# A transformer layer on one core: the first keys by halves of tokens, the second term order for their sums, GpSimd's pair output one normalisation later, and a routing step moved at the change of stage

## What is computed

```python
# x: (8, 512, 256); all float32
h = layernorm(x); xn = h / norm(h) * sqrt(256) * (gamma + 1)
q, k, v = split(xn @ w_qkv)                    # 16 heads of 64
attn = softmax((q / 8) @ k.T); x = x + merge(attn @ v) @ w_out
h = layernorm(x)
p = softmax(h @ router_w); top = top_k(p, 2); top = top / sum(top)
x = x + (gelu(h @ w1 + b1) @ w2 + b2) * sum(top)
```

## Time and profile before

| | before |
|---|---|
| median of 3 runs | 1160.66 us (1159.94 to 1162.03) |
| the profiled execution | 1159.99 us |
| its span, first to last instruction | 1158.2 us |
| TensorE busy | 1146.1 us, 99% of the span |
| VectorE / ScalarE / GpSimd busy | 87% / 76% / 58% |
| granted TensorE clock in the records | 1.000 |

### The profile page before, as it was taken

The page is one execution under the profiler, slowest core; times in us unless marked ns, Lnnn a source line. Parts: engine busy times, 40 slices in busy tenths (PEclk is TensorE's granted clock), DMA queues, the critical chain, the costliest instruction groups (busy, mean ns, idle before and its releaser), DMA issues.

```text
span 1158.2 us, 26395 instructions
## 1 busy us (share of the span) xinstructions
PE 1146.1 (99%) x9923; PEld 951.4 (82%) x9923; DVE 1006.8 (87%) x1767; ACT 874.8 (76%) x1896; POOL 666.6 (58%) x827
## 2 busy tenths in 40 slices
PE   9999999999999999999999999999999999999999
PEld 6778888888888888888888888888888877788887
DVE  6889888988888888888888888888988988889985
ACT  6888888888888888888888888888888885334432
POOL 6786566655666565656565656565656585323421
DMA  4224112311231123112221213121312135334321
GB/s 124 75 80 110 34 37 70 90 33 36 74 92 38 38 74 92 38 38 74 70 60 37 74 56 75 37 70 31 92 33 67 43 110 152 129 112 141 116 75 38
DMA packets 58270, 82.92 MB, mean 72 GB/s; under 512 B 12576, under 2 KB 34592, under 8 KB 58144
## 3 DMA queue, kind: packets, MB, share of 16 engines
q1 hardware_dynamic: 58144, 81.24, 25.6%
HBM read 31.14 MB, written 16.25 MB: 41 GB/s over the span
## 4 chain that ended last, share of the span: by engine, by line
PE 91%; DVE 2%; ACT 1%; issue 0%; POOL 0%; DVEq 0%; ACTq 0%; POOLq 0%
PE ps L615 34%; PE ps L696 19%; PE ps L681 12%; PE ps L642 10%; PE ps L648 5%; PE ps L854 4%; PE ps L858 2%; PE ps L767 1%; PE ps L766 1%; PE ps L725 1%; PE ps L824 1%; PE ps L859 1%; DVE pT_lo L1207 0%; DVE f_o L1451 0%; POOL pT_hi L1087 0%
## 5 line engine op out<-in xcount | busy, mean ns | idle before, releaser
L1078 POOL TENSOR_SCALAR prob<-prob,rowinv 128x512 f32<-128x512 f32 x512 | 353.2, 703 | 334.0 <-DVE rowinv L1296 333.9
L1207 DVE TENSOR_TENSOR pT_lo<-ps,pT_hi 128x512 fp32r<-128x512 f32 (+1 forms) x384 | 320.5, 862 | 57.7 <-ACT pT_hi L976 57.1
L983 ACT ACTIVATE prob<-ps,negmax 128x512 f32<-128x512 f32 x512 | 347.3, 688 | 16.3 <-DVE negmax L1291 11.8
L1291 DVE TENSOR_REDUCE negmax<-ps 128x2 f32<-128x1024 f32 x256 | 305.8, 1215 | 1.3 <-PE ps L648 1.2
L973 ACT ACTIVATE pT_hi<-ps 128x1024 fp32r<-128x1024 f32 x128 | 131.3, 1026 | 112.4 <-issue 111.0
L681 PEld LDWEIGHTS ps<-identity,prob 64*128 64x128 f32 x4096 | 157.5, 138 | 67.8 <-issue 44.3
L681 PE MATMUL ps<-identity,prob 64*128 64x64 f32 x4096 | 175.6, 225 | 3.2 <-DVE pT_lo L1207 2.1
L642 PE MATMUL ps<-nat 64*128 64x512 f32 x1024 | 170.9, 411 | 1.4 <-ACT prob L983 1.1
L615 PE MATMUL ps<-xT_hi,wbig 128*128 128x512 f32 x514 | 166.6, 405 | 0.2 <-DVE pT_lo L1207 0.2
L976 ACT ACTIVATE pT_hi<-ps 128x512 fp32r<-128x512 f32 x256 | 139.3, 596 | 8.8 <-PE ps L681 0.6
L696 PE MATMUL ps<-pT_hi,vbuf 128*128 128x512 f32 x512 | 138.4, 392 | 0.9 <-DVE pT_lo L1207 0.9
(11 more groups left out here) (116 smaller groups left out, 1988.9 us busy)
## 6 DMA issues: line engine op xcount, KB each, us to landing
att_hi_v<-halves_out SPq DMA_DIRECT2D x128, 128.0 KB, 2.3
att_lo_v<-halves_out SPq DMA_DIRECT2D x128, 128.0 KB, 2.4
blocks_scratch<-xblocks SPq DMA_DIRECT2D x15, 512.0 KB, 2.8
xn<-blocks_scratch SPq DMA_DIRECT2D x60, 128.0 KB, 2.9
xin<-in_x SPq DMA_DIRECT2D x32, 128.0 KB, 3.0
xres<-in_x SPq DMA_DIRECT2D x8, 512.0 KB, 3.5
x_scratch<-xres SPq DMA_DIRECT2D x8, 512.0 KB, 3.3
xin<-x_scratch SPq DMA_DIRECT2D x32, 128.0 KB, 3.2
```

Of the source, the lines that this page charges most:

```text
L983: act.activation(prob[:, n % NPROB, j * SEQ:(j + 1) * SEQ], ps[:, PS_SCORE[n % 2] + j, :], ACT.Exp, bias=negmax[:, n % 4, j:j + 1], accum_ ...
L1078: return pool.tensor_scalar(dst, src, scalar, 1.0, ALU.mult, ALU.mult)
L1207: return dve.tensor_tensor(dst, full, hi, ALU.subtract)
L1291: dve.tensor_reduce(negmax[:, n % 4, :], ps[:, PS_SCORE[n % 2]:PS_SCORE[n % 2] + 2, :], AX.X, ALU.max, negate=True).then_inc(s_max, 1)
```

## The change

Five edits.

1. The transposes of the first xn go by halves of tokens: ("xt", 0) is tokens 0 to 255 for both channel groups, in banks 0 and 1, ("xt", 1) the rest, in banks 7 and 3. ScalarE's and VectorE's parts of xT come in four pieces of 256 columns each, with semaphores of their own. The first keys are two products of 256 tokens, and each product's terms go hi x hi, then weights-hi x xT_lo, then weights-lo x xT_hi (before: weights-lo second).
2. `gain` (128x2) and the low part of first weights 0 move from VectorE to GpSimd, behind its second `powers`. The single matmul of zeros in step -3 is gone.
3. The high part of the values' first weights (`first_weights(2)`) moves on ScalarE from behind the second piece to between the two pieces of the first queries.
4. GpSimd's `attention_out` of pairs 0 to 61 moves from behind `normalise_prob(4p+8)` to behind `normalise_prob(4p+9)`, the next tile. Pairs 62 and 63 stay.
5. At the change of stage VectorE's `turn_logits(1)` stands ahead of `base(0)`, `routing_shift(1)` ahead of the last two output blocks, `routing_weight(1)` behind `turn_input`, and the two `finish` of chunk 0 behind the hidden blocks f = 1 and f = 4 of chunk 1.

```diff
-WARM = {FIRST_STEP: 12, -3: 1}
+WARM = {FIRST_STEP: 12}
+PS_XT = ((0, 1), (7, 3))
 # TensorE
-                for i, j in ((0, 0), (1, 0), (0, 1)):
+                halves_in = 1 if queries.stop <= SEQ // 2 else 2
+                for i, j in ((0, 0), (0, 1), (1, 0)):
                     if (i, j) == (0, 0):
                         pe.wait_ge(s_first_hi, 1)
                     if i == 1:
-                        pe.wait_ge(s_first_lo, 1)
+                        pe.wait_ge(s_first_lo_pool, 1)
                     for k in range(KT):
-                        if j == 0:
-                            pe.wait_ge(s_auxhi, aux_index[("xt", k)] + 1)
-                        else:
-                            pe.wait_ge(s_aux, done_no("xt", k))
+                        pe.wait_ge(s_xt_lo if j else s_xt_hi, KT * (halves_in - 1) + k + 1)
...
-                    for t in range(TT):
-                        if k == 0:
-                            pe.wait_ge(s_xn_first, t + 1)
-                        ins = pe.transpose(bank[:, t * P:(t + 1) * P], xn[:, t, k * P:(k + 1) * P],
-                                           identity[:, :])
+                    for t in (2 * half, 2 * half + 1):
+                        pe.wait_ge(s_xn_first, t + 1)
+                        for k in range(KT):
+                            ins = pe.transpose(ps[:, PS_XT[half][k], t * P:(t + 1) * P], xn[:, t, k * P:(k + 1) * P],
+                                               identity[:, :])
...
-                        ins = first_product(bank, base, slice(0, SEQ))
+                        for half in range(2):
+                            tokens = slice(half * SEQ // 2, (half + 1) * SEQ // 2)
+                            ins = first_product(bank[:, tokens], base, tokens)
 # ScalarE
+                    for k in range(KT):
+                        act.activation(xT[0][:, k, tokens], ps[:, PS_XT[args[0]][k], tokens], ACT.Copy, scale=gain[:, k:k + 1])\
+                            .then_inc(s_xt_hi, 1)
...
                             .then_inc(s_q_first_hi, 1)
+                        first_weights(2)
                         act.wait_ge(s_auxfull, block_no + 1)
...
-                for g in {FIRST_SLOT + 2: (0,), -7: (1, 2)}.get(slot, ()):
+                for g in {FIRST_SLOT + 2: (0,), -7: (1,)}.get(slot, ()):
 # GpSimd
+                if pair_at(step - 2) is not None and step < STEPS:
+                    attention_out(pair_at(step - 2))
                 task = ln_task(2 * step - 1)
...
                     powers(1, slice(2, TT))
+                    pool.wait_ge(s_const, 16 * N_CONST)
+                    pool.tensor_scalar(gain[:, :], gamma_sb[:, :], 1.0, 1.0, ALU.add, ALU.mult).then_inc(s_gain, 1)
+                    first_lo(0)
...
-                if pair_at(step - 1) is not None:
+                if pair_at(step - 1) is not None and step == STEPS:
                     attention_out(pair_at(step - 1))
 # VectorE
+                    for k in range(KT):
+                        dve.wait_ge(s_xt_hi, KT * args[0] + k + 1)
+                        lo(xT[1][:, k, tokens], ps[:, PS_XT[args[0]][k], tokens], xT[0][:, k, tokens], gain[:, k:k + 1])\
+                            .then_inc(s_xt_lo, 1)
...
-                if slot == -10:
-                    dve.wait_ge(s_first_hi, 1)
-                    lo(first_parts[0][1], first_stage[0], first_parts[0][0]).then_inc(s_first_lo, 1)
...
-                            dve.tensor_scalar(gain[:, :], gamma_sb[:, :], 1.0, None, ALU.add).then_inc(s_gain, 1)
...
+                    if c == 1 and f in (1, TT):
+                        finish(0, f // TT)
                 if c >= 1:
                     base(c)
                 if c == 0:
                     routing_shift(0)
                     routing_weight(0)
+                    turn_logits(1)
                     base(0)
...
-                if c + 1 < B:
+                if 1 <= c < B - 1:
                     turn_logits(c + 1)
                 if c == 0:
+                    routing_shift(1)
                     for block_of_out in last_out:
                         aux_done(*block_of_out)
...
-                if c + 1 < B:
+                if c == 0:
+                    routing_weight(1)
+                elif c + 1 < B:
                     routing_shift(c + 1)
-                finish(c, 0)
+                if c >= 1:
+                    finish(c, 0)
```

More of the change, by code:

```diff
@@ L138, in layer_kernel @@
     out_tasks = [task for task in aux_index if task[0] == "out"]
-    other_tasks = [task for task in aux_index if task[0] != "out"]
+    other_tasks = [task for task in aux_index if task[0] not in ("out", "xt")]
     x_v = x.rearrange("b (p t) d -> b p t d", t=TT)
@@ L731, in aux @@
                 begun = kind == "k" and any(block[2] == "out" for block in aux_of(step)[0])
-                same_bank = [j for j in range(block_no) if aux_bank(j) == aux_bank(block_no)]
+                same_bank = [task for task in other_tasks
+                             if aux_index[task] < block_no and aux_bank(aux_index[task]) == aux_bank(block_no)]
                 if begun:
@@ L936, in aux_hi @@
                 if kind == "xt":
-                    k, = args
+                    tokens = slice(args[0] * SEQ // 2, (args[0] + 1) * SEQ // 2)
                     act.wait_ge(s_gain, 1)
-                    ins = act.activation(xT[0][:, k, :], bank, ACT.Copy, scale=gain[:, k:k + 1])
+                    for k in range(KT):
+                        act.activation(xT[0][:, k, tokens], ps[:, PS_XT[args[0]][k], tokens], ACT.Copy, scale=gain[:, k:k + 1])\
+                            .then_inc(s_xt_hi, 1)
+                    return
                 elif kind == "q":
@@ L1226, in aux_done @@
                     lo(nat[:, 0, QL, 0:P], ps[:, PS_Q_FIRST, 0:P], nat[:, 0, QH, 0:P], SCALE).then_inc(s_q_first, 1)
-                dve.wait_ge(s_auxhi, hi_no)
                 if kind == "xt":
-                    k, = args
-                    ins = lo(xT[1][:, k, :], bank, xT[0][:, k, :], gain[:, k:k + 1])
-                elif kind == "q":
+                    dve.wait_ge(s_gain, 1)
+                    tokens = slice(args[0] * SEQ // 2, (args[0] + 1) * SEQ // 2)
+                    for k in range(KT):
+                        dve.wait_ge(s_xt_hi, KT * args[0] + k + 1)
+                        lo(xT[1][:, k, tokens], ps[:, PS_XT[args[0]][k], tokens], xT[0][:, k, tokens], gain[:, k:k + 1])\
+                            .then_inc(s_xt_lo, 1)
+                    return
+                dve.wait_ge(s_auxhi, done_no(kind, *args))
+                if kind == "q":
                     part = nat[:, args[0] % 2]
@@ L1351, in slot_tasks @@
                             ins.then_inc(s_xn, 1)
-                        if step == 8 and b == 0:
-                            dve.wait_ge(s_const, 16 * N_CONST)
-                            dve.tensor_scalar(gain[:, :], gamma_sb[:, :], 1.0, None, ALU.add).then_inc(s_gain, 1)
             for step in range(FIRST_STEP, LAST_STEP + 2):
@@ L1489, in _ @@
                     turn_input(1)
-                if c + 1 < B:
+                if c == 0:
+                    routing_weight(1)
+                elif c + 1 < B:
                     routing_shift(c + 1)
-                finish(c, 0)
-                if c + 1 < B:
+                if c >= 1:
+                    finish(c, 0)
+                if 1 <= c < B - 1:
                     routing_weight(c + 1)
-                finish(c, 1)
+                if c >= 1:
+                    finish(c, 1)
 def kernel(**inputs):
```

36 lines of the change are left out of this document (20 added, 16 removed).

## The result

| | before | after |
|---|---|---|
| median | 1160.75 us (1159.90 to 1162.03, 22 runs) | 1162.49 us (1161.24 to 1163.57, 22 runs) |
| ratio, 95% interval | | 1.0014 (1.0008 to 1.0020) |
| the profiled execution, its span | 1159.99, 1158.2 us | 1163.23, 1161.3 us |
| mean granted clock of an execution | 1.000 in all | 1.000 in 11, 0.999 in 11 |

The change costs 1.7 us (0.9 to 2.3 by the interval), and the forecast was 0.2 us faster than the median of three.

The account below looks back on a forecast made before the run. TensorE was taken as the bound, busy 1146.1 of 1158.2 us. 1159.99 - 0.4 (head) + 0.2 (stage) + 0 (pair output) = 1159.8 us; the profiled run lies 0.67 below the median, so 1160.5 us, range 1159.4 to 1161.6.

Parts of the forecast that it names:

- the change of stage: Chunk 1: two TensorE waits for gelus (0.68 and 0.43 us) become one of about 2 us; cost 0.2 us.
- Pair output: GpSimd's attention output one normalisation later, 62 pairs: worth 0, cost 0, bound 0.05 us a pair.
- over 1 us to spare: GpSimd's later-input steps: work behind the pair output at most 0.4 us later, the following tile having this margin.
- The rival with this sign: Moved pair output gains after all: 0.05 us on 62 pairs, 3 us, giving 1157.4 us; chance 0.03.
- Head: Start of the kernel: first keys' high part at 10.15 us against 10.53, gain 0.4 us, bounds 0.15 to 0.8.
- the collision: In the head: GpSimd's 1.29 us low part of weights 0 getting in front of VectorE's last xn tile.
- the first rival: In the head, GpSimd precedes VectorE's last xn tile: keys at 11.05, 0.5 us later, total 1161.4 us; chance 0.24.
- The spread's data: Change of stage: SP's spread of xn, starting at 997.4, lands at 1001.4 to 1001.8 us, holding up x2_hi(2).
- The clock: In the head, TensorE's clock falls back to 1.2 GHz: 2.65 us more, total 1163.1 us; chance 0.09.

Follow-up runs that it names:

- E3: Kernel before with only VectorE's new order at the change of stage: 1162.13 us, ratio 1.0010.
- E2: Kernel before with only GpSimd's pair output one normalisation later: 1160.16 us, ratio 0.9994.
- E12: Kernel before with the pair's output later only where GpSimd's high part of the next batch's input follows (seven of 64 pairs): 1160.28 us, ratio 0.9990.
- E1: Kernel before with only the head's edits; pair output and stage change as before: 1161.05 us, ratio 1.0003.
- E7: Changed kernel with x2_hi(2) behind the sixth gelu of chunk 1 and GpSimd's first low weights waiting for all four xn tiles: 1162.16 us, ratio 1.0008.
- E4: Changed kernel with one wait more: GpSimd's low part of the first weights starts only behind the last xn tile: 1161.29 us, ratio 1.0009.
- E9: E4 with VectorE's two sums of the last output blocks moved behind the turned blocks: 1160.47 us, ratio 0.9994.
- E6: Changed kernel with nine extra dummy products on TensorE in its 2.63 us wait before up(1,6): 1161.89 us, ratio 1.0008.
- E11: E4 with the old stage order, except both parts of finish(0) behind low parts f = 1 and f = 4 of chunk 1: 1160.30 us, ratio 0.9993.
- E10: E4 with both parts of finish(0) back in front of chunk 1's low parts, router's logits and shift still early: 1162.11 us, ratio 1.0007.
- E5: Changed kernel with x2_hi(2) and its low part behind the sixth gelu of chunk 1, not the fourth: 1162.58 us, ratio 1.0014.

## Why the prediction was wrong, step by step

Three steps failed, and the largest is the change of stage: priced at +0.2 us, measured at +0.85 us in E3's profile, with about 0.7 us more in the median by the fall of the clock.

**Pair output: 0, measured about -0.6 us (E2, not clear of noise by itself) and -1.0 us (E12, clear of it).** The step "worth 0, since nobody waits for that tile" was read from a pair in the middle and from a view of waits of one execution. For the steps with a later input's high part the prediction had "over 1 us to spare". In the old order the first of them had about 0.1: GpSimd's wait was 0.55 us longer in E3 than in before and 1.21 longer in E1, and the step lost 0.45 and 1.1. In before's execution the halves landed 0.99 us after GpSimd was free; in E1's they landed 2.20 us after it, and the step lost 1.1 us. The move protects that step against a late landing, though not wholly (E7 lost 0.26 us). The prediction had the clue that its profiled execution lay 0.67 us below the median, and treated this as spread without asking what is late in the others. The rival with this sign was bounded by 0.05 us for each of 62 pairs, so the place was wrong and not only the size.

**Head: -0.4, measured +0.6 in the profile.** Without the collision (E4) the keys' high part came at 10.16, forecast 10.15, and with it at 11.19, where the first rival had 11.05, with the long xn row that it named. The first agreement is partly luck: E4's xn began 0.18 us earlier than before's, and the same program gave 10.67 in E9. In the mean of the profiles the head without the collision is worth 0.2 us, half of the forecast. What failed was the choice: a margin of hundredths of a microsecond was given 0.42 against 0.24 in the chances. By the profiles it falls on either side, and alone the head came out at +0.25 us, not separable from nothing.

The Trainium skill (SBUF — State Buffer, section "SBUF: two separate sides") says that VectorE and GpSimd share a port pair, which one of them holds for a whole instruction while the other is blocked. The sizes agree: the tile took 1.45 us, 1.04 more than its 0.41, beside a low part of 1.26. By the page whichever starts first gets the pair. By the recorded starts the tile was first, by 0.04 us, so these don't tell who gets it.

**Change of stage: +0.2, measured +1.3 alone by the medians and +0.85 by E3's profile.** The mechanism inside chunk 1 stood as forecast: gelu 8 at once, blocks turned 0.90 us later (994.02 less 0.58 for the later start, against 992.54 before), one wait of 1.80 us in E3 and 2.63 in after for the forecast of about 2. In E3, chunk 1 took 0.21 us more, the forecast 0.2. Three terms were mis-sized or missing.

*The spread's data.* The forecast was 1001.4 to 1001.8, and `x2_hi(2)` started at 1003.06. Of the 1.3 us and more between them, 0.58 are the head's. The rest is the store: from SP's store to its spread it was 2.64 us in before and in E3, 3.53 in after and 3.38 in E4, so that its landing varies by up to 0.9 us, in a place where each tenth goes to the end.

*VectorE's debt.* The prediction put `finish` at 0.96 us each and the last low part of chunk 1, due at 1009.5, at 1008.7, and it stopped looking at the end of chunk 1. Each of the two moved parts is four instructions and takes 1.9 us, as before's own trace has it:

```profile
994.38 1.91 DVE L1451 SCALAR_TENSOR_TENSOR f_o<-ps,r_weight,f_o 128x256 f32<-128x256 f32 x4
```

In E3 the second part starts at 1006.13, the last three low parts follow it, and `base(1)` behind them starts at 1010.10, or 1009.5 without the 0.64 us that E3 was late at the start. So the forecast reserve of 0.8 us was not there, and 0.67 us fall in chunk 2 (E3, E4, E6, E9, E11). That half the price of `finish` is all of the difference wasn't tested.

*The clock.* The rival was priced at 2.65 us but put in the head. There it didn't come true, and the first products, in 4.49 us in after against 5.49 in before, don't tell of the change: over all profiles the same products took 4.44 to 5.49 us with the new head and 4.69 to 5.49 with the old. The clock fell behind the wait that the prediction itself had forecast at the change of stage. With 11 of 22 executions it moves the median from 1161.79 to 1162.49 us, by 0.7; the executions with a fall are 1.2 us longer by their medians.

**Sum.** By the single runs: -0.6 (E2) + 0.25 (E1) + 1.3 (E3) + 0.7 (clock) = 1.65 us, measured 1.74. Each of the first three has an interval of about 1 us either way, so that the agreement to a tenth is luck. For the profiled execution: 0.58 us from the head and 15.38 - 12.79 = 2.59 us in chunk 1 are the 3.1 us of the span. Chunk 2's 0.67 us did not come in it, nor in E10 (22.96 us), the other one with a low clock inside chunk 1; E6, with the clock kept up, has it, which fits that the slow clock gave VectorE the time.

What stays open: why the halves and the store land about 1 us apart from run to run; how much of before's spread is the loss at 115 us, since it was seen only in the profiles of E1, E3 and, small, E7; and from which wait on the clock falls. The expectation of E3 put that at some 2 us. No run shows such a bound: behind 2.53 us it stayed in one profile and behind 2.55 it fell in another.

## What to carry to other kernels

Two short waits and one long one of the same sum need not cost the same: here the clock could fall behind a TensorE wait of 2.5 us, so ask for the granted clock behind the long one, and count the instructions of a moved block before pricing it. An engine that is 87% busy and moved work later has a debt, and the next chunk's waits show it, so compare the chunk behind the one that was changed. Where an execution lies below its median, look for what lands late in the others, and put a step that depends on a DMA behind work that is ready.

## What the runs showed of the hardware

- The granted clock behind a wait of TensorE's at this place: 0.50 to 0.51 for about 3 us with waits of 2.63 (after), 2.74 (E5) and 2.77 us (E10), and a mean of 0.998 in the profile with 2.55 us (E7); 1.00 behind 1.80 (E3) and 2.53 us (E4's profile; four of E4's other ten executions have 0.999). After 2.20 us of dummy products and a wait of 0.55 (E6) it stayed at 1.00.
- A VectorE tile of 128x256 that takes 0.41 us took 1.45 and 1.47 where a GpSimd subtraction of 128x512 started 0.04 and 0.06 us behind it (after, E6), and 0.41 where that started 0.14 and 0.18 us behind it (E5, E1); there the subtraction took 1.40 and 1.35 us and not 1.27.
- From the issue of a store of 512 KB to the load that waits for it: 2.64 to 2.85 us in ten of the fourteen profiles, 3.22 to 3.53 in the other four (E7, E4, E6, after).
- GpSimd's wait for the regrouped halves of one pair was 0.99, 1.54 and 2.20 us in three executions with the same program up to there but for the head (before, E3, E1).
